# A decoder of attentions and routed experts: the combine stages are folded into the attentions that follow

## The chip, the cores and the metric

The kernel runs on one core of a Trainium2 chip as one launch. The metric is the device time of that launch in microseconds (us), the median of several executions. Engines are named as the profile does: PE is TensorE, PEld its weight load, DVE is VectorE, ACT is ScalarE, POOL is GpSimd, and SP is the queue that issues most DMAs. "L712" is line 712 of the kernel before.

## What is computed

`x` is 16 batches of 112 tokens with 256 channels, and `ctx` has 375 context tokens for each batch. Eight blocks follow each other, each added to `x`:

```
x = x + attention_L0(layernorm(x), ctx)   # 16 heads of 16, biases, a mask of keys for each query
x = x + experts_L0(layernorm(x))          # 2 of 8 experts per token, relu
x = x + attention_L1(layernorm(x), ctx)   # one head of 256, relu in place of softmax
x = x + block_L1(layernorm(x))            # y = layernorm(x) + causal self attention with rotary
                                          # angles; y + 2 of 8 experts, capacity 448, gelu
x = x + attention_L2(layernorm(x), ctx)   # 16 heads of 64, no biases
x = x + experts_L2(layernorm(x))          # 1 of 8 experts per token, relu
x = x + attention_L3(layernorm(x), ctx)   # 16 heads of 64, biases, output bias of 256
x = x + experts_L3(layernorm(x))          # all 16 experts and a shared one, weighted
```

An expert layer's output for a token is the sum of its chosen experts' rows, each times the token's gate.

## The kernel before

`x` stays in SBUF as 112 partitions by 16 batches by 256. Each stage is an `nc.Block()`: every engine runs its own list of instructions for the stage, ordered against the others by counting semaphores alone, and no engine goes into the next block before all have left this one.

The stages of an expert layer of L0, L1 and L2 are three. `route` normalises, scores and picks experts, computes for each token its place in a table of slots (`core.slot_out`) and its gate (`core.gate`), and POOL scatters the normalised rows to `slots_in` in DRAM. `expert_tiles` runs the experts over tiles of slots and stores the results to `slots_out`. `combine` gathers them back: for each of 16 batches POOL issues one indirect DMA (L1548) per chosen expert into one of 8 `got` buffers, and DVE multiplies by the gate and adds to `x` (L1559). Ahead of L2 and L3, SP also loads the next attention's four weights of 1 MB in `combine` (L1539), into buffers that live for `combine` and the attention only.

`cross_attention` serves L0 (narrow: heads of 16) and L2 and L3 (wide: heads of 64). Its unit is a step of one batch, in 16 sub-steps of one head. In the step of batch b, PE computes the scores of each head, transposes the probabilities of three heads back ("turn", L508), multiplies them with the values (L523), and puts a piece of other work in between, from a table written out by hand (`order`): keys K0 to K7, values V0 to V5 and queries of batch b+1, and the output projection Y0 and Y1 of batch b-1 (L459). With an output bias, PE adds it as one more matmul of a row of ones with the bias row (L462). DVE takes each head's maximum (L826), ACT the exponent (L676), POOL the reciprocal of the sum and the product (L710, L712). At sub-step 0 DVE runs `normalise_start` of batch b+1 (L741 to L745), and then the lower halves of K0 and K1 (L770), for which PE's K2 waits in sub-step 1; POOL raises the variance to -1/2 (L704, L732), and `normalise_end` is in sub-step 2. Ahead of the first step of a wide attention DVE splits the weights (L918, L920) and two contexts (L808, L810) into high and low halves.

`relu_attention` has shorter steps: DVE normalises batch b+1 (L978 to L982, POOL L1801, DVE L1931) at the step's start, while PE computes scores of b and keys of b+1 (L1815); then PE transposes the normalised tokens (L1823).

In `self_attention`'s step DVE does, in this order: `divide(b-1)`, `group_max(b, 2)`, `spread_keys(b+1)` (L2320), `norm_3(b+2)` (L2285), `group_max(b, 3)` (L2328), and the rest. `norm_3` writes the normalised tokens that PE transposes at L2068; ACT's exponents (L2233) of group 3 wait for the last maximum.

Most batches of these three functions run in hardware loops of two batches a turn (`Fori`); the first and the last ones are written out.

Of the kernel before, what the change touches and what calls it, by code (L numbers as in the profile page):

```python
# [123 lines left out]
def cross_attention(nc, core, name, ctx_in, w, dh, mask=None):  # L124
# [39 lines left out]
    with ctx:  # L164
# [82 lines left out]
        nweights = 4 + (4 if biased else 0) + (3 if mask else 0)  # L247
# [63 lines left out]
        def run(heads, first, last, tail, engine):  # L311
# [11 lines left out]
        with nc.Block() as block:  # L323

            @block.sync
            def _(sp):
# [3 lines left out]
                if biased:  # L330
                    for dst, src in ((bq, w["bq"]), (bk, w["bk"]), (bv, w["bv"]), (bo, w["bo"])):
                        sp.dma_start(dst[:, :], src).then_inc(weights.sem, 16)
# [9 lines left out]
                if wide:  # L342
# [10 lines left out]
                    with sp.Fori(0, (B - 2) // 2) as i:  # L353
                        next_ctx(Batch(i, 2))
                        next_ctx(Batch(i, 3))
# [31 lines left out]
                with sp.Fori(0, (B - 2) // 2) as i:  # L387
                    spread(Batch(i, 0))
                    next_load(Batch(i, 2))
                    spread(Batch(i, 1))  # L390
                    next_load(Batch(i, 3))
                spread(Batch(0, B - 2))
                spread(Batch(0, B - 1))
# [4 lines left out]
            def _(pe):  # L398
                def piece(p, b, slot):
# [53 lines left out]
                    else:  # L453
# [4 lines left out]
                        for c in range(EC):  # L458
                            ins = pe.matmul(bank[0:T, 0:YW], oT[:, c, :], wo[:, c, m * YW:(m + 1) * YW],  # L459
                                            start=(c == 0), stop=(c == EC - 1 and not biased))  # L460
# [141 lines left out]
                pe.wait_ge(weights.sem, weights.at(16 * nweights))  # L602
# [9 lines left out]
            def _(act):  # L612
                act.preload_act_table(ACT.Exp)

                act.wait_ge(weights.sem, weights.at(16 * nweights))
# [84 lines left out]
            def _(pool):  # L700
# [5 lines left out]

                def weigh(b, h):
# [21 lines left out]
                with pool.Fori(0, B - 1) as i:  # L729

# [1866 lines left out]
```

## Time and profile before

| | us |
|---|---|
| median of 3 runs | 3820.91 (3817.61 to 3829.95) |
| the profiled execution's own time | 3808.83 |
| its span, first to last instruction | 3807.0 |
| PE busy | 3181.0 (84%) |
| DVE busy | 1563.8 (41%) |
| ACT busy | 1538.9 (40%) |
| POOL busy | 1223.3 (32%) |

The profile is of one execution. The busy share of an engine is a mean over stages with different limits, so stages are read one by one. In the rows below, times are from the span's start; what stands in brackets at a row's end is the idle time of the engine before it, and what ended that time.

### The profile page before, as it was taken

How to read it: one execution, taken by the hardware profiler on the slowest of the kernel's cores; microseconds unless marked ns; L12 is line 12 of the kernel's file. 1: busy time of each engine (PE TensorE's matmuls, PEld its weight loads, DVE VectorE, ACT ScalarE, POOL GpSimd, SP SyncE). 2: the span in 40 equal slices, each digit the busy share in tenths (PEclk: the TensorE clock that was granted, in tenths of full speed). 3: DMA queues.
4: the chain of work that ended last, by engine and by line, in shares of the span. 5: the costliest groups of instructions: out<-in, count | busy, mean ns of one | idle time of the engine just before them, and what ended most of it. 6: DMA issues, size and time to landing. Idle time of an engine off the chain costs nothing. (4 is left out here: it accounts for less than half of the span.)

```text
span 3807.0 us, 67515 instructions
## 1 busy us (share of the span) xinstructions
PE 3181.0 (84%) x22302; PEld 2618.4 (69%) x22302; DVE 1563.8 (41%) x3515; ACT 1538.9 (40%) x4385; POOL 1223.3 (32%) x1334
## 2 busy tenths in 40 slices
PE   2899927993978837948999999759599999996998
PEld 2777727883856625636888888648478888885998
DVE  2777730002456530024444444310244444444776
ACT  1555513441345522214555555324255555552222
POOL 0000030003000030034676676510166666664121
PEclk8999958997989958978999999779799999996999
DMA  6555418982100014330000000058400000000001
GB/s 181 129 130 138 104 37 291 321 307 73 44 13 0 0 35 144 115 93 17 9 12 8 8 8 5 3 204 311 132 10 8 8 8 12 8 1 14 26 26 33
DMA packets 155225, 287.93 MB, mean 76 GB/s; under 512 B 53214, under 2 KB 126876, under 8 KB 137244
## 3 DMA queue, kind: packets, MB, share of 16 engines
q1 hardware_dynamic: 147420, 267.93, 23.1%
q0 software_dynamic: 7680, 18.36, 1.8%
q8 instruction: 75, 1.23, 0.1%
q14 instruction: 50, 0.41, 0.0%
HBM read 240.88 MB, written 45.35 MB: 75 GB/s over the span
## 5 line engine op out<-in xcount | busy, mean ns | idle before, releaser
L712 POOL TENSOR_SCALAR L_probs<-L_probs,L_inverse 112x375 f32<-112x375 f32 x512 | 645.7, 1261 | 87.1 <-issue 87.1
L826 DVE TENSOR_REDUCE L_negmax<-bank 112x1 f32<-112x375 f32 x768 | 394.7, 542 | 427.2 <-PE bank L481 361.4
L676 ACT ACTIVATE L_probs<-bank,L_negmax 112x375 f32<-112x375 f32 x768 | 434.5, 571 | 204.9 <-DVE L_negmax L826 199.7
L508 PE MATMUL bank<-ident,L_probs 112*125 112x112 f32 x2304 | 400.6, 283 | 17.6 <-POOL L_probs L712 11.3
L508 PEld LDWEIGHTS bank<-ident,L_probs 112*125 112x125 f32 x2304 | 336.3, 188 | 93.0 <-issue 62.0
L710 POOL TENSOR_TENSOR L_inverse<-L_sums,neg_one 112x1 f32<-112x1 f32 x512 | 308.1, 602 | 256.4 <-ACT L_probs L676 256.4
L656 ACT ACTIVATE L_probsT<-bank 125x336 f32<-125x336 f32 x512 | 231.6, 452 | 263.0 <-PE bank L508 263.0
L638 ACT ACTIVATE v<-bank 125x512 f32<-125x512 f32 x192 | 114.7, 598 | 266.1 <-PE bank L431 266.1
L523 PE MATMUL bank<-L_probsT,v 125*64 125x112 f32 x3072 | 206.1, 270 | 1.1 <-ACT L_probsT L656 1.1
L523 PEld LDWEIGHTS bank<-L_probsT,v 125*64 125x64 f32 x3072 | 150.8, 137 | 30.7 <-DVE L_oT L842 2.0
L1484 ACT ACTIVATE L0t_hidden<-bank,L0t_b 128x128 f32<-128x128 f32 x280 | 102.8, 367 | 165.3 <-PE bank L1444 146.1
L1444 PE MATMUL bank<-L0t_xT,L0t_w 128*128 128x128 f32 x1120 | 134.2, 279 | 22.9 <-DMA L0t_b<-in_F_b 22.5
L676 ACT ACTIVATION_READ_ACCUMULATOR L_probs<-bank,L_negmax 112x1 f32 x768 | 152.7, 199 | 0.0
L1444 PEld LDWEIGHTS bank<-L0t_xT,L0t_w 128*128 128x128 f32 x1120 | 130.3, 194 | 31.7 <-issue 31.0
L424 PE MATMUL bank<-L_ctx_hi,L_wk_hi 128*128 128x376 f32 x512 | 146.9, 368 | 3.3 <-DVE L_keys_lo L770 3.0
L1505 DVE TENSOR_TENSOR L0t_ys<-bank,L0t_b 128x256 f32<-128x256 f32 x35 | 14.8, 424 | 314.3 <-PE bank L1456 314.3
L431 PE MATMUL bank<-L_wv_hi,L_ctx_hi 128*125 128x512 f32 x384 | 137.9, 440 | 0.0
L770 DVE SCALAR_TENSOR_TENSOR L_keys_lo<-bank,L_bk,L_keys_hi 128x376 fp32r<-128x376 f32 x128 | 76.6, 608 | 141.1 <-ACT L_keys_hi L628 141.0
L732 POOL TENSOR_TENSOR L_stats<-L_stats,neg_half 112x1 f32<-112x1 f32 x15 | 8.1, 542 | 381.5 <-DVE L_stats L745 381.5
L459 PE MATMUL bank<-wo,L_oT 128*112 128x128 f32 x1024 | 128.7, 281 | 1.6 <-DVE L_oT L842 0.8
L424 PE MATMUL bank<-L_ctx_hi,L_wk_lo 128*128 128x376 f32 x512 | 129.8, 334 | 0.0
L416 PE MATMUL bank<-L_hT,wq 128*128 128x112 f32 x1024 | 128.4, 280 | 1.0 <-ACT L_hT L626 1.0
(291 smaller groups left out, 6995.8 us busy)
## 6 DMA issues: line engine op xcount, KB each, us to landing
L0t_w<-in_F_w SPq DMA_DIRECT2D x70, 1024.0 KB, 5.3
L2t_w<-in_F_w SPq DMA_DIRECT2D x42, 1024.0 KB, 5.2
L_keys<-spread_k SPq DMA_DIRECT2D x64, 376.0 KB, 6.4
L_ctxT<-in_ctxT SPq DMA_DIRECT2D x48, 375.0 KB, 3.3
L1t_w<-in_F_w SPq DMA_DIRECT2D x16, 1024.0 KB, 6.1
slots_in<-zeros SPq DMA_DIRECT2D x4, 1792.0 KB, 16.5
L_q<-spread_q SPq DMA_DIRECT2D x128, 56.0 KB, 2.2
spread_k<-L_k_hi SPq DMA_DIRECT2D x16, 376.0 KB, 2.5
```

What stands on the lines that cost most here:

```text
L416: ins = pe.matmul(bank[:, (c - 4 * m) * T:(c - 4 * m + 1) * T], wq[:, k, c * P:(c + 1) * P], hT[:, k, :], start=(k == 0), stop=(k == DC - 1))
L424: ins = pe.matmul(bank[:, 0:SP], wt[:, k, m * P:(m + 1) * P], c[b.par][:, k, :], start=(n + k == 0), stop=(n + k == DC + 1))
L431: ins = pe.matmul(bank[0:SJ, 0:VW], c[b.par][:, k, j * SJ:(j + 1) * SJ], wt[:, k, vn * VW:(vn + 1) * VW], start=(n + k == 0), stop=(n + k ...
L459: ins = pe.matmul(bank[0:T, 0:YW], oT[:, c, :], wo[:, c, m * YW:(m + 1) * YW], start=(c == 0), stop=(c == EC - 1 and not biased))
L508: ins = pe.transpose(psT[h % len(psT)][0:SJ, j * T:(j + 1) * T], probs[h % NB][:, j * SJ:(j + 1) * SJ], core.ident[0:T, 0:T])
L523: ins = pe.matmul(bank[i * dh:(i + 1) * dh, at:at + T], v[b.par][0:SJ, j, (h + i) * dh:(h + i + 1) * dh], probsT[(h + i) % NT][:, j, :], s ...
L656: act.activation(probsT[h % NT][:, :, :], psT[h % len(psT)][0:SJ, 0:J * T].rearrange("p (j t) -> p j t", t=T), ACT.Copy)\
L676: act.activation(probs[e % NB][:, :], psS[e % 2][0:T, 0:S], ACT.Exp, bias=negmax[b.par][:, e:e + 1], accum_out=sums[b.par][:, e:e + 1]).th ...
L710: pool.tensor_tensor(inverse[b.par][:, h:h + 1], sums[b.par][:, h:h + 1], core.neg_one[0:T, :], ALU.pow)
L712: pool.tensor_scalar(probs[h % NB][:, :], probs[h % NB][:, :], inverse[b.par][:, h:h + 1], None, ALU.mult)\
L826: dve.tensor_reduce(negmax[b.par][:, h:h + 1], psS[h % 2][0:T, 0:S], AX, ALU.max, negate=True).then_inc(maxed.sem, 1)
L1444: ins = pe.matmul(psH[f % 4][:, 0:tile], w1[t.par][:, k, f * P:(f + 1) * P], xT[:, k, :], start=(k == 0), stop=(k == DC - 1))
```

## The change

- `combine` is gone, three stages in all. `relu_attention` and the wide `cross_attention` gather and add themselves: four `got` buffers, the gathers of four batches at the start of the stage, then the gathers of batch b+4 in step b (in `relu_attention` behind the power of b, in a wide attention ahead of head 8). DVE's `add_experts` adds a batch's rows directly ahead of that batch's `normalise_start`. An attention L2 step so has two more indirect DMAs on POOL and two more DVE operations, an L3 step one of each.
- The 4 MB of weights of the next wide attention are loaded in `route` of the expert layer before, behind its own loads, into buffers held from there on, with a counter of their own.
- The output bias of L0 and L3 is broadcast to 112 partitions when it is loaded, and POOL adds it to `x` (`bias_x`), once a batch: in L3 ahead of head 5 and in L0 behind the next batch's power. The matmuls L462 go; DVE's addition of Y waits for `x_biased`. POOL waits for the stage's weights first where there are biases.
- In `self_attention`, `norm_3(b+2)` stands directly behind `divide(b-1)`.
- The loops of `cross_attention`, `relu_attention` and `self_attention` are written out for all 16 batches (not POOL's loop in `self_attention`).

```diff
@@ cross_attention
-            bo = sb("bo", [1, D])
+            bo = sb("bo", [T, D])
+            x_biased = core.counter("x_biased")
+        if wide:
+            wide_weights = core.counter("wide_weights")
+            got = [sb(f"got{r}", [T, topk, D]) for r in range(4)]
...
-            with engine.Fori(0, (B - 4) // 2) as i:
-                heads(Batch(i, 1), False, False)
-                heads(Batch(i, 2), False, False)
-            heads(Batch(0, B - 3), False, False)
+            for n in range(1, B - 2):
+                heads(Batch(0, n), False, False)
...
-                        if biased:
-                            ins = pe.matmul(bank[0:T, 0:YW], core.ones[0:1, 0:T], bo[0:1, m * YW:(m + 1) * YW],
-                                            start=False, stop=True)
...
+                def bias_x(b):
+                    pool.wait_ge(normed_ready.sem, normed_ready.at(b.n + 1))
+                    xb = core.x[:, b.n, :]
+                    pool.tensor_tensor(xb, xb, bo[:, :], ALU.add).then_inc(x_biased.sem, 1)
...
+                        if h == 5 and biased:
+                            bias_x(b)
+                        if h == 8 and b.n + 4 < B:
+                            gather(b.n + 4)
                         weigh(b, h)
+                def gather(n):
+                    if n >= 4:
+                        pool.wait_ge(added.sem, added.at(n - 3))
+                    for k in range(topk):
+                        pool.indirect_dma_start(
+                            out=got[n % 4][:, k, :], out_offset=None, in_=core.slots_out[:, :],
+                            in_offset=bass.IndirectOffsetOnAxis(ap=core.slot_out[:, k, n:n + 1], axis=0))\
+                            .then_inc(gathered[n % 4].sem, 16)
+                if biased:
+                    pool.wait_ge(weights.sem, weights.at(16 * nweights))
                 if wide:
+                    for n in range(4):
+                        gather(n)
                     run(heads, rstd, None, lambda b: None, pool)
...
+                def add_experts(n):
+                    dve.wait_ge(gathered[n % 4].sem, gathered[n % 4].at(16 * topk * (n // 4 + 1)))
+                    for k in range(topk):
+                        ins = dve.scalar_tensor_tensor(out=core.x[:, n, :], in0=got[n % 4][:, k, :],
+                                                       scalar=core.gate[:, k, n:n + 1], in1=core.x[:, n, :],
+                                                       op0=ALU.mult, op1=ALU.add)
+                        if k == topk - 1:
+                            ins.then_inc(added.sem, 1)
+                        dve.drain()
                 def normalise_start(b):
+                    if wide:
+                        add_experts(b.n)
                     dve.bn_stats(stats[:, 0:6], x_of(b))
...
@@ route, sync
+                for dst, s in next_loads:
+                    sp.dma_start(dst, s).then_inc(core.counter("wide_weights").sem, 16)
@@ combine
-def combine(nc, core, name, topk, next_loads=()):
...
@@ self_attention, vector
                     if prior:
                         divide(b + -1)
+                    if after2:
+                        norm_3(b + 2)
                     group_max(b, 2)
                     if after:
                         spread_keys(b + 1)
-                    if after2:
-                        norm_3(b + 2)
                     group_max(b, 3)
```

`relu_attention` gets the same `gather` and `add_experts`, and calls `add_experts(b.n + 1)` ahead of `normalise_start`.

## Rows read from the trace of the kernel before

**Rows 1.** A stretch of time by engine: busy (instructions), TensorE clock, DMA share, GB/s.

```profile
200.00:460.00 260.00, 237.50 (x2228) 193.84 (x2227) 197.00 (x467) 140.33 (x430) 5.41 (x10) 1.00 0.55 130
1120.00:1320.00 200.00, 176.04 (x983) 121.47 (x981) 120.66 (x266) 114.33 (x502) 12.44 (x23) 0.93 0.00 0
1800.00:2100.00 300.00, 300.00 (x2359) 245.82 (x2358) 136.69 (x275) 159.30 (x441) 207.79 (x227) 1.00 0.03 9
```

**Rows 2.** Order of time, border from the first combine to relu attention: start, length.

```profile
867.32 0.96 POOL L1548 DMA_INDIRECT L0c_got<-slots_out,slot_out  x1 [293.93 <-PEq L1534]
...
910.03 0.35 SPq L1781 DMA_DIRECT2D L1x_wq<-in_X_wq  x1
...
920.76 1.59 PE L1815 MATMUL bank<-L1x_ctxT,L1x_wk 128*128 128x375 f32 x2 [56.91 <-DMA L1x_ctxT<-in_ctxT]
```

**Rows 3.** Order of time, border from the second combine to attention L2.

```profile
1667.30 0.37 SPq L1539 DMA_DIRECT2D v<-in_L_wk  x1
...
1712.13 14.73 SPq L344 DMA_DIRECT2D L_ctxT<-in_ctxT  x3
...
1726.02 0.42 DVE L741 BATCH_NORM_STATS2 L_stats<-x 112x6 f32<-112x256 f32 x1
```

**Rows 4.** Order of time, border from the third combine to attention L3.

```profile
2692.11 0.35 SPq L1539 DMA_DIRECT2D v<-in_L_wk  x1
...
2714.94 0.33 SPq L332 DMA_DIRECT2D L_bq<-in_L_bq  x1
```

**Rows 5.** Instructions on the second combine's tile: ns min/median/max, first and last start.

```profile
L1548 POOL DMA_INDIRECT L1c_got<-slots_out,slot_out x32: 929/934/1136, 1668.0 to 1707.0; - x32
L1559 DVE SCALAR_TENSOR_TENSOR x<-L1c_got,gate,x x32: 475/484/542, 1676.7 to 1711.1; 112x256 f32<-112x256 f32 x32
```

**Rows 6.** One line's instructions, attention L2, the batches inside the loop.

```profile
L741 DVE BATCH_NORM_STATS2 L_stats<-x x11: 415/417/419, 1838.9 to 2274.2; 112x6 f32 x11
```

**Rows 7.** The same line, attention L3, the batches inside the loop.

```profile
L741 DVE BATCH_NORM_STATS2 L_stats<-x x11: 415/416/418, 2847.0 to 3294.0; 112x6 f32 x11
```

**Rows 8.** Order of time, VectorE, a batch of attention L2 outside the loop.

```profile
2361.22 0.41 DVE L741 BATCH_NORM_STATS2 L_stats<-x 112x6 f32<-112x256 f32 x1
```

**Rows 9.** Order of time, TensorE, output projection in attention L3.

```profile
3002.35 1.26 PE L459 MATMUL bank<-wo,L_oT 128*112 128x128 f32 x10
...
3003.94 0.58 PE L508 MATMUL bank<-ident,L_probs 112*125 112x112 f32 x3
```

**Rows 10.** Order of time, TensorE, output projection in attention L0.

```profile
295.95 1.03 PE L459 MATMUL bank<-L_wo,L_oT 128*112 128x256 f32 x4
...
297.52 0.37 PE L494 MATMUL bank<-L_barred,ident_b 112*112 112x376 bf16 x1
```

**Rows 11.** Order of time, VectorE, start of a batch's step in attention L2.

```profile
2013.78 0.15 DVE L745 TENSOR_SCALAR L_stats<-L_stats 112x1 f32<-112x1 f32 x1
2014.31 1.18 DVE L770 SCALAR_TENSOR_TENSOR L_keys_lo<-bank,L_keys_hi 128x376 fp32r<-128x376 f32 x2 [0.38 <-ACT L_keys_hi L628]
```

**Rows 12.** The same moment on TensorE.

```profile
2015.36 0.61 PE L424 MATMUL bank<-L_ctx_hi,L_wk_hi 128*128 128x376 f32 x2
```

**Rows 13.** Order of time, one step of relu attention.

```profile
958.40 0.41 DVE L1931 TENSOR_SCALAR L1x_normed<-x,L1x_stats 112x256 f32 x1 [0.65 <-POOL L1x_stats L1801]
...
960.03 0.36 PE L1823 MATMUL bank<-ident,L1x_normed 112*128 112x112 f32 x2
```

**Rows 14.** Order of time, one step of self attention at full clock.

```profile
1246.78 0.41 DVE L2285 TENSOR_SCALAR L1s_normed<-y,L1s_stats 112x256 f32 x1
...
1247.42 0.38 PE L2068 MATMUL bank<-ident,L1s_normed 112*128 112x112 f32 x2 [1.62 <-DVE L1s_normed L2285]
...
1247.75 0.35 ACT L2233 ACTIVATE L1s_probs<-bank,L1s_negmax 112x112 f32<-112x112 f32 x1 [1.12 <-DVE L1s_negmax L2328]
```

**Rows 15.** GpSimd's line in attention L2's last batch.

```profile
L710 POOL TENSOR_TENSOR L_inverse<-L_sums,neg_one x16: 567/568/572, 2405.2 to 2434.4; 112x1 f32<-112x1 f32 x16
```

**Rows 16.** GpSimd's groups: busy us, mean ns; idle before.

```profile
L1621 POOL TENSOR_TENSOR L3d_w_lo<-L3d_raw,L3d_w_hi 128x768 fp32r<-128x768 f32 x18 | 33.6, 1869 | 2.6
```

More of the change, by code:

```diff
@@ L246, in cross_attention @@
         taken = {c: core.counter(f"taken_{c}") for c in "LQKVOY"}
-        nweights = 4 + (4 if biased else 0) + (3 if mask else 0)
+        nweights = (0 if wide else 4) + (4 if biased else 0) + (3 if mask else 0)
+        if wide:
+            wide_weights = core.counter("wide_weights")
+            got = [sb(f"got{r}", [T, topk, D]) for r in range(4)]
+            gathered = [core.counter(f"gathered{r}") for r in range(4)]
+            added = core.counter("added")
         if wide:
@@ L352, in _ @@
                     next_ctx(Batch(0, 1))
-                    with sp.Fori(0, (B - 2) // 2) as i:
-                        next_ctx(Batch(i, 2))
-                        next_ctx(Batch(i, 3))
+                    for n in range(2, B):
+                        next_ctx(Batch(0, n))
                     return
@@ L386, in _ @@
                 load(Batch(0, 1))
[L387 to L393, printed above, removed]
+                for n in range(B):
+                    spread(Batch(0, n))
+                    if n + 2 < B:
+                        next_load(Batch(0, n + 2))
                 sp.wait_ge(core.zeroed_sem, 16 * (core.slots_in.shape[0] // (B * T)))
@@ L728, in _ @@
                 rstd(Batch(0, 0))
-                with pool.Fori(0, B - 1) as i:
-                    pool.wait_ge(var_ready.sem, var_ready.at(i + 2))
-                    pool.tensor_tensor(stats[:, 9:10], stats[:, 8:9], core.neg_half[0:T, :], ALU.pow)\
-                        .then_inc(rstd_ready.sem, 1)
+                for n in range(B):
+                    if n + 1 < B:
+                        rstd(Batch(0, n + 1))
+                    bias_x(Batch(0, n))
             @block.vector
@@ L776, in take @@
                     dve.wait_ge(made[p[0]].sem, made[p[0]].at(count(p, b)))
+                    if p[0] == "Y" and biased:
+                        dve.wait_ge(x_biased.sem, x_biased.at(b.n + 1))
                     if p[0] == "Y":
@@ L943, in cross_attention @@
             w_split.stage_over(2)
+            wide_weights.stage_over(64)
+            added.stage_over(B)
+            for r in range(4):
+                gathered[r].stage_over(16 * topk * (B // 4))
             ctx_split.stage_over(B)
@@ L1750, in relu_attention @@
         weightsT = sb("weightsT", [SJ, J, T])
+        got = [sb(f"got{r}", [T, topk, D]) for r in range(4)]
+        gathered = [core.counter(f"gathered{r}") for r in range(4)]
+        added = core.counter("added")
         weights = core.counter("weights")
@@ L1768, in run @@
             heads(Batch(0, 0), False)
-            with engine.Fori(0, (B - 2) // 2) as i:
-                heads(Batch(i, 1), False)
-                heads(Batch(i, 2), False)
+            for n in range(1, B - 1):
+                heads(Batch(0, n), False)
             heads(Batch(0, B - 1), True)
@@ L1926, in _, with add_experts @@
                 dve.wait_ge(weights.sem, weights.at(16 * len(loads)))
+                def add_experts(n):
+                    dve.wait_ge(gathered[n % 4].sem, gathered[n % 4].at(16 * topk * (n // 4 + 1)))
+                    for k in range(topk):
+                        ins = dve.scalar_tensor_tensor(out=core.x[:, n, :], in0=got[n % 4][:, k, :],
+                                                       scalar=core.gate[:, k, n:n + 1], in1=core.x[:, n, :],
+                                                       op0=ALU.mult, op1=ALU.add)
+                        if k == topk - 1:
+                            ins.then_inc(added.sem, 1)
+                        dve.drain()
                 def normalise_end(b):
@@ L1973, in relu_attention @@
             s.stage_over(16 * B // 2)
+        added.stage_over(B)
+        for s in gathered:
+            s.stage_over(16 * topk * (B // 4))
         for s in (var_ready, rstd_ready, normed_ready, scored, mixed, made["L"], taken["L"], made["Q"], taken["Q"],
@@ L2034, in run @@
             heads(Batch(0, 0), False, True, True, True)
-            with engine.Fori(0, (B - 4) // 2) as i:
-                heads(Batch(i, 1), True, True, True, True)
-                heads(Batch(i, 2), True, True, True, True)
-            for n in range(B - 3, B):
+            for n in range(1, B):
                 heads(Batch(0, n), True, n + 1 < B, n + 2 < B, n + 3 < B)
```

124 lines of the change are left out of this document (55 added, 69 removed).

## The prediction

> **What bounds the kernel now.** I read the kernel by stages, first by stretches of time. In the steady part of the wide attentions PE is busy all the time at the full clock, 300 us of 300 [rows 1]; in attention L0 it is busy 237.5 of 260 us, and in self attention 176 of 200 with a granted clock of 0.93 [rows 1]. So work taken from PE counts there, and work given to DVE or POOL costs only what makes PE wait. Then I read the borders in order of time. A combine stage leaves PE idle: it had waited 56.9 us when relu attention's first matmul started [rows 2]. The reader should see that no other work lies beside a combine, so its whole length, border included, is on the path.
>
> **What is removed.** From the first gather of the first combine (867.32) to relu attention's first load (910.03) is 42.7 us [rows 2]; from SP's first weight load (1667.30) to L2's first context load (1712.13), 44.8 [rows 3]; for the third, 22.8 [rows 4]. Together -110.3. The 4 MB of weights move to `route`, behind its own loads on SP's queue, and are needed over 200 us later; I cost them at nothing. Their cover is `route`, where PE and DVE work on data in SBUF; without it they would cost what their bytes take.
>
> The bias matmuls L462. In L3 the last of ten projection matmuls ends at 3003.61, and the next work starts at 3003.94 [rows 9]; matmuls in a row start before the one ahead ends, so at least 0.33 us per piece goes. From the other side, an L3 batch takes (3294.0 - 2847.0) / 10 = 44.70 us and an L2 batch (2274.2 - 1838.9) / 10 = 43.53 [rows 6, 7]: 1.17 for two pieces, but L3's other biases are in it. I take the middle, 0.46: 32 pieces, -14.7 (bounds -10.6 and -18.7). In L0 the gap behind four matmuls is 297.52 - 296.98 = 0.54 [rows 10], up to 0.80 with one matmul's share of the 1.03; at 0.6 it is -9.6 for 16 batches. Bounds are 0, if the queries' way through DRAM and not PE sets L0's step, and -12.8.
>
> **What is added at the starts.** A gather takes POOL (1707.0 - 1668.0) / 31 = 1.26 us and a DVE addition 0.48, two with what lies between them about 1.1 [rows 5]. Eight gathers are 10.1 us of POOL. In relu attention PE started 10.7 us after the stage [rows 2], so the first power, behind them in POOL's queue, is about in time, and the addition lies under the first keys. The gathers' 0.9 MB share the DMA engines with some 1.8 MB of loads: 0 to +5.4 (10.7 x 0.9 / 1.8); I take +1.5, since a queue of many small loads rarely fills them. In L2 and L3 the normalisation starts 13.9 us after the stage (1726.02 - 1712.13) [rows 3], and the gathers are over by then; the additions stand on the path: +1.1 in L2, +0.6 in L3, and +0.3 for the wider bias load. Sum +3.5.
>
> **What is added to the steps.** Wide attention: DVE's additions stand ahead of `normalise_start`, and behind that stands the lower half of K0, for which PE's K2 waits. L745 ends at 2013.93; the two L770 start at 2014.31, so the first ends near 2014.90, and K2 starts at 2015.36 [rows 11, 12]. Shifted by 1.12, DVE is free at 2015.05 and K0 done at 2015.64; with the 0.23 us that PE starts after DVE's end where it does wait (1247.19 to 1247.42 [rows 14]), or a third of that where only its queue waits, K2 starts at 2015.7 to 2015.9. I take +0.35 for 14 batches, +4.9; L3, with one addition, +0.1, +1.4 (bounds 0, and the whole 1.12 and 0.56: +23.5). What is late next is all behind K2, since PE has no idle time to give back.
>
> POOL in a wide step needs (2434.4 - 2405.2) / 15 = 1.95 us a head [rows 15], 31.1 a batch; with the power of the variance (0.57, as L710) and two gathers (2.5) 34.2 of 43.5. A product is needed three heads, some 8 us, later; behind the gathers wait heads 8 and 9, 2.5 us late. Hidden. Only in the last batch, where PE has no pieces left, POOL runs without a pause and sets the pace [rows 15]; L3's `bias_x` stands there. No row shows an addition of 112x256 on POOL: bounds are 0.57 (112x1, L710) and 1.87 (128x768, L1621 [rows 16]); in proportion 1.0. So +1.0.
>
> Relu attention: the normalised tokens are ready at 958.81, PE takes them at 960.03 [rows 13]; less 0.23, the slack is 0.99 against the addition's 1.12: +0.13, +2 for 15 batches (bounds 0, +16.8).
>
> Self attention: PE waits 1.62 us for `norm_3` [rows 14]. But ahead of the second maximum it delays that maximum, the exponents, the queries and `spread_keys` by about 0.35 (its start to the next operation's), and the last maximum gets the same 0.35 back; ACT's exponents, which wait for that maximum [rows 14], start when they did. ACT then runs through to the tokens that PE's next projection needs, so PE's wait moves instead of going. What may go is the low clock: 0.93 over 200 us means 28 us at 1.2 GHz [rows 1], at most 14 us lost over the stretch and 16 over the stage. I take -3 (bounds +5, -16).
>
> Loops: a batch outside the loop starts (2361.22 - 2274.2) / 2 = 43.5 after the one before, like inside [rows 6, 8]. Cost 0. The Trainium skill, in Runtime: NRT & Kernel Launch, "Instruction fetch mechanics", says that a taken branch can force a fetch before execution goes on, and that kernels prefer unrolling. By it the loops' edges would hold something to win; the rows show none, so the sum stays.
>
> **The sum.** -110.3 - 14.7 - 9.6 + 3.5 + 4.9 + 1.4 + 1.0 + 2 - 3 = -124.8, from the profiled execution's own 3808.8 to 3684. The median of the runs lies 12.1 above that execution; taken from it, the forecast is 3696 us.
>
> **Rivals.**
> (a) The additions stand on the path in full, since DVE's order, not the slack, decides: relu 16.8 and wide 23.5 instead of 8.3, +32: 3728. For it: DVE's operations wait for PE and ACT at many places of a step. Against: PE's full use is at the matmuls' own pace, and DVE is busy 137 of 300 us [rows 1]. 0.12.
> (b) POOL becomes the wait in the wide steps. It decides from 8 us of delay, that is if a pair of gathers cost 8 instead of 2.5; then heads 8 and 9 hold up PE. At 10 us, in L3 with `bias_x` in it, 2 us for 12 batches and two stages: +48, 3744. Against: 0.93 us each, with DVE at work beside them, and at most 1.14 [rows 5]. 0.04.
> (c) DVE locks POOL out at the start of a wide stage. DVE splits weights and contexts there; if each gather waits for what DVE runs, POOL's queue grows from 10.1 by DVE's some 11 us of work to 21, and the first power comes 5 us late in L2 and 2 in L3: 3703. The Trainium skill, SBUF — State Buffer, "Who interferes with whom", says that a DVE copy or cast in two-port mode keeps GpSimd from writing descriptors; by its example of 3.1 us instead of 0.62, eight gathers would take 25 us, an estimate, and L2 start 9 us late. No row here shows gathers beside casts. 0.06.
> (d) The clock in self attention comes back in full, since PE's longest wait in the step goes: -13 more: 3683. 0.13.
> (e) The bias matmuls' time isn't won, since POOL's `x_biased` or L0's other chain takes their place: +24: 3720. 0.07.
> (f) Slower than before: written-out code is fetched too late. 62 batches leave their loops (12 in four stages, 14 in relu attention), so it decides from 125 / 62 = 2.0 us per batch more; at 3 us it is +186: 3882. Against it the batches outside the loop [rows 8]. 0.02.
> The forecast has 0.56.
>
> **How the numbers follow.** Its own range is 3680 to 3712: L0's and L3's bounds down, half of the steps' upper bounds up. With (a), (d), (e) and (c) inside, 3674 to 3730 leaves out about 2 in 10, with the spread of the runs. Under 0.3% (11 us), about what a measurement of this kernel can tell from no change, only (f) comes near: faster 0.97, same 0.01, slower 0.02.
>
> **What would show it.** PE's gap at the three borders: about 15, 22 and 22 us. L741's spacing: about 43.9 in L2 and 43.9 in L3, so nearly alike; above 44.5 in L2 speaks for (a). L0's steps 0.6 shorter. POOL's gathers near 0.93 in the first 15 us of L2; over 2 for (c). Self attention's clock over 0.93 for (d), and the wait at L2068 gone while one at L2077 comes. Wrong would be made the forecast by a new wait of over 1 us in each wide step, since there are 30.

## The result and the profile after

The changed kernel takes 3703.0 us (median of 4 runs, 3701.7 to 3705.0), beside 3819.3 for the kernel before on the same chip: a ratio of 0.970, 95% interval 0.968 to 0.972. The prediction was 3696 (3674 to 3730), faster with 0.97. The profiled execution has a span of 3703.1 us, 103.9 less than before.

I cut both traces at TensorE's first and last matmul of each stage (in attention L0 at the first batch's first scores matmul). The two columns are single executions.

| part | before | after | change | predicted |
|---|---|---|---|---|
| attention L0 | 413.5 | 410.8 | -2.7 | -9.6 |
| routing's last matmul to the end of L0's expert tiles | 338.8 | 352.5 | +13.7 | 0 |
| border to relu attention | 56.9 | 15.0 | -41.9 | -41.2 |
| relu attention | 146.8 | 147.9 | +1.1 | +2 |
| self attention | 268.4 | 254.8 | -13.6 | -3 |
| border to L2 | 65.0 | 21.9 | -43.1 | -43.7 |
| attention L2 | 718.7 | 727.5 | +8.8 | +4.9 |
| routing's last matmul to the end of L2's tiles | 207.6 | 214.5 | +6.9 | 0 |
| border to L3 | 44.6 | 24.8 | -19.8 | -21.9 |
| attention L3 | 738.9 | 721.7 | -17.2 | -12.3 |
| all others | | | +3.9 | 0 |

The borders came as forecast: "about 15, 22, 22" were 15.0, 21.9 and 24.8. Three lines were not: L0 gained little, self attention much, and the expert tiles, in which nothing was changed, took 20.6 us more.

Stretches of time of the changed kernel, the counterparts of [rows 1] (us busy, instructions; then the clock, the DMA engines' share and GB/s):

```profile
200.00:460.00 260.00, 231.89 (x2215) 191.98 (x2214) 197.35 (x470) 140.32 (x430) 13.18 (x21) 1.00 0.56 132
1090.00:1290.00 200.00, 177.01 (x1071) 124.86 (x1070) 126.73 (x282) 122.75 (x550) 12.96 (x24) 1.00 0.00 1
1750.00:2050.00 300.00, 298.87 (x2342) 244.81 (x2342) 137.47 (x287) 158.87 (x441) 217.41 (x240) 1.00 0.06 16
```

In self attention the granted clock is now 1.00, where it was 0.93: that is 2.4 GHz all the time. In L2 PE is idle 1.1 of 300 us, where it had not been idle at all.

The start of a batch's normalisation on VectorE in steady L2 and L3 (ns min/median/max, first and last start), the counterparts of [rows 6, 7]:

```profile
L779 DVE BATCH_NORM_STATS2 L_stats<-x x14: 427/428/429, 1716.4 to 2285.5; 112x6 f32<-112x256 f32 x14
```

```profile
L779 DVE BATCH_NORM_STATS2 L_stats<-x x13: 427/428/429, 2760.5 to 3282.9; 112x6 f32<-112x256 f32 x13
```

L2's step is (2285.5 - 1716.4) / 13 = 43.78 us, +0.25 against 43.53. L3's is (3282.9 - 2760.5) / 12 = 43.53, -1.17 against 44.70.

The border to relu attention in order of time, beside [rows 2]:

```profile
878.49 0.96 POOL L1806 DMA_INDIRECT L1x_got<-slots_out,slot_out  x1 [307.32 <-POOLq L1414]
...
888.21 1.05 DVE L1949 SCALAR_TENSOR_TENSOR x<-L1x_got,gate,x 112x256 f32<-112x256 f32 x2 [12.61 <-DMA L1x_maskT<-in_X_maskT]
...
890.09 2.21 PE L1832 MATMUL bank<-L1x_ctxT,L1x_wk 128*128 128x375 f32 x3 [15.05 <-DMA L1x_ctxT<-in_ctxT]
```

Eight gathers take 9.7 us (878.49 to 888.13), each 0.93 to 0.96, and VectorE's additions end at 889.26, before the first keys' matmuls, which wait for the context's load: the addition is under cover, as the prediction had it.

The border to L2, beside [rows 3]. This is where rival (c) is to be looked for:

```profile
1625.30 1.23 DVE L960 CAST L_wk_hi<-v 128x2048 fp32r<-128x2048 f32 x1 [3.77 <-PEq L1414]
1625.98 1.38 POOL L738 DMA_INDIRECT L_got<-slots_out,slot_out  x1 [236.30 <-POOLq L1414]
1626.61 2.29 DVE L962 TENSOR_TENSOR L_wk_lo<-v,L_wk_hi 128x2048 fp32r<-128x2048 f32 x1
...
1630.46 2.77 POOL L738 DMA_INDIRECT L_got<-slots_out,slot_out  x1 [0.30 <-issue]
...
1635.24 0.93 POOL L738 DMA_INDIRECT L_got<-slots_out,slot_out  x1 [0.31 <-issue]
...
1638.14 0.55 DVE L848 CAST L_ctx_hi<-L_ctxT 128x752 fp32r<-128x752 f32 x1 [4.02 <-DMA L_ctxT<-in_ctxT]
...
1639.63 1.05 DVE L769 SCALAR_TENSOR_TENSOR x<-L_got,gate,x 112x256 f32<-112x256 f32 x2
...
1642.93 0.60 PE L410 MATMUL bank<-ident,L_normed 112*128 112x112 f32 x2 [21.87 <-DVE L_normed L788]
```

A gather's issue takes 1.38 us, 2.49 and 2.77 while VectorE splits weights, and 0.93 when VectorE waits (1635.24). So the mechanism of (c) is there: "over 2 for (c)" came true. Its price did not: TensorE starts 21.9 us after the tiles, as forecast without it. The power on GpSimd comes at 1641.77, right behind VectorE's statistics; what is late is VectorE, which waits 4.02 us for the second context, ahead of the first batch's addition. The Trainium skill, SBUF — State Buffer, "Who interferes with whom", says that VectorE and GpSimd share a port pair under an exclusive lock. That gathers get longer beside VectorE's work agrees with it (2.77 beside 0.93); the lock itself no trace here shows.

The border to L3, beside [rows 4]:

```profile
2624.20 0.35 SPq L337 DMA_DIRECT2D L_bq<-in_L_bq  x1
...
2625.54 0.43 SPq L337 DMA_DIRECT2D L_bo<-in_L_bo  x1
2626.02 18.19 SPq L349 DMA_DIRECT2D L_ctxT<-in_ctxT  x3
2629.16 1.23 DVE L960 CAST L_wk_hi<-v 128x2048 fp32r<-128x2048 f32 x1 [7.11 <-DMA L_bo<-in_L_bo]
...
2642.07 0.55 DVE L848 CAST L_ctx_hi<-L_ctxT 128x752 fp32r<-128x752 f32 x1 [3.90 <-DMA L_ctxT<-in_ctxT]
...
2643.56 0.48 DVE L769 SCALAR_TENSOR_TENSOR x<-L_got,gate,x 112x256 f32<-112x256 f32 x1
...
2646.30 0.60 PE L410 MATMUL bank<-ident,L_normed 112*128 112x112 f32 x2 [24.82 <-DVE L_normed L788]
```

VectorE's first split waits for L_bo, the bias row broadcast to 112 partitions: it starts 3.1 us after the issue of the context's load (2626.02), where the kernel before had it 0.9 after (2716.63 and 2717.52 in its trace). That is 2.2 us for which I had 0.3.

### The profile page after: what moved, and what is told of

The parts are those of the page before. It is cut to its first block and busy times, and to the rows that moved or that the text cites. A ratio compares the mean times of both kernels' runs of the same rounds, so it can differ in the third digit from the quotient of the medians.

```text
span 3703.1 us, 62003 instructions
## 1 busy us (share of the span) xinstructions
PE 3152.0 (85%) x22206; PEld 2606.9 (70%) x22206; DVE 1554.8 (42%) x3515; ACT 1537.1 (42%) x4385; POOL 1248.5 (34%) x1366
## 5 line engine op out<-in xcount | busy, mean ns | idle before, releaser
L718 POOL TENSOR_TENSOR L_inverse<-L_sums,neg_one 112x1 f32<-112x1 f32 x512 | 297.0, 580 | 147.2 <-ACT L_probs L678 146.7
L706 POOL TENSOR_TENSOR L_stats<-L_stats,neg_half 112x1 f32<-112x1 f32 x48 | 26.9, 561 | 538.8 <-DVE L_stats L783 538.8
L738 POOL DMA_INDIRECT L_got<-slots_out,slot_out x48 | 57.4, 1196 | 442.5 <-POOLq L1414 236.3
L521 PEld LDWEIGHTS bank<-L_probsT,v 125*64 125x64 f32 x3072 | 152.4, 138 | 30.4 <-ACT L_probsT L658 1.6
L1806 POOL DMA_INDIRECT L1x_got<-slots_out,slot_out x32 | 30.5, 953 | 315.3 <-POOLq L1414 307.3
## 6 DMA issues: line engine op xcount, KB each, us to landing
slots_in<-zeros SPq DMA_DIRECT2D x4, 1792.0 KB, 16.3
```

The source lines that it names most:

```text
L521: ins = pe.matmul(bank[i * dh:(i + 1) * dh, at:at + T], v[b.par][0:SJ, j, (h + i) * dh:(h + i + 1) * dh], probsT[(h + i) % NT][:, j, :], s ...
L718: pool.tensor_tensor(inverse[b.par][:, h:h + 1], sums[b.par][:, h:h + 1], core.neg_one[0:T, :], ALU.pow)
```

## The experiments

Twelve runs, one of them (e5) of the changed kernel again. "Ratio" is to the kernel before on the same chip, with its 95% interval; the changed kernel's own is 0.9697 (0.9678 to 0.9716). Since the runs used several chips, differences between kernels are taken from the ratios, times 3819 us. The stages are cut as in the table.

**e1, norm_3 back.** The last edit of the diff undone:

```
+                    group_max(b, 2)
+                    if after:
+                        spread_keys(b + 1)
                     if after2:
                         norm_3(b + 2)
-                    group_max(b, 2)
-                    if after:
-                        spread_keys(b + 1)
```

> The changed kernel with one edit undone: in self attention's step norm_3 stands behind spread_keys again. In the traces the self attention stage took 268.4 us from its first to its last matmul before the change and 254.8 after it, 13.6 less, and the granted clock had no dip in it afterwards. Theory (the move gives the clock back): the stage goes back to about 268, dips of the clock return, and the time is about 13 us above the changed kernel's 3703, so 3716. Rival (the dips of the kernel before were chance, or came from what ran ahead of the stage, so the move gives only what I forecast for it, 3 us): the stage takes about 258 and the time is 3706.

3711.2 us, ratio 0.9730 (0.9714 to 0.9747), so 12.6 us slower than the change, though the two intervals still touch; the stage takes 265.3. A stretch of its self attention:

```profile
1100.00:1300.00 200.00, 175.23 (x1011) 122.56 (x1010) 120.84 (x263) 117.05 (x521) 11.89 (x22) 0.95 0.00 1
```

0.95 where the change has 1.00. In the clock's record of this kernel eight dips of 3.4 us to half speed lie inside the stage, and seven with two of 6.8 in the kernel before; the changed kernel has none after the first 30 us. The theory holds, rival (d) of the prediction. What a dip costs is read from the steps of one batch. Two steps of this kernel without a dip:

```profile
1250.67 0.41 PE L2098 MATMUL bank<-ident,L1s_normed 112*128 112x112 f32 x2 [1.58 <-DVE L1s_normed L2315]
...
1266.00 0.41 PE L2098 MATMUL bank<-ident,L1s_normed 112*128 112x112 f32 x2 [1.57 <-DVE L1s_normed L2315]
```

Such a step takes 15.33 us, and one with a dip in it some 16.55, so eight dips are about 10 us. The stage is 10.5 longer than the change's; its steps without a dip are longer too (e12), and against that its clock was low for a shorter time near the start.

**e12, the same edit alone on the kernel before.**

> The kernel before with one part of the change alone: norm_3 first in self attention's step. Undone in the changed kernel, it cost 10.5 us of that stage (254.8 to 265.3), with the granted clock down from 0.98 to 0.94. Theory: self attention goes from 268.4 to about 256 us, the clock in its steady part from 0.93 to 0.98, and the time from 3819 to 3807. Rival (the clock's gain needed something else of the change, as what runs ahead of the stage): 265 us, 3816.

3811.6 us, ratio 0.9968 (0.9944 to 0.9992): 12 us faster, with an interval of 3 to 21 that holds both the theory's 12 and the rival's 4. Its stage took 264.7 in the profile, which is the rival's number, but not for the rival's reason:

```profile
1145.00:1345.00 200.00, 173.35 (x1054) 122.36 (x1053) 123.52 (x267) 122.81 (x546) 11.89 (x22) 1.00 0.00 0
```

The steady part is at 1.00, without a dip. A part of what it lost lies at the stage's ends, 17.1 us of 1.2 GHz near the start and 9.1 at the end. Another part lies in the steps. The weight loads of the two transposes of each step, in e12 and in the change (ns min/median/max, first and last start):

```profile
L2068 PEld LDWEIGHTS bank<-ident,L1s_normed x24: 138/143/146, 1147.7 to 1315.4; 112*128 112x128 f32 x24
```

```profile
L2098 PEld LDWEIGHTS bank<-ident,L1s_normed x22: 139/140/141, 1104.8 to 1254.9; 112*128 112x128 f32 x22
```

That is (1315.4 - 1147.7) / 11 = 15.25 us a step in e12, which keeps the loops, and (1254.9 - 1104.8) / 10 = 15.01 in the change, where they are written out; with the old order a step without a dip is 15.33 written out (e1, e3) and 15.26 to 15.35 in loops (the kernel before). In the eleven executions with the new order the stage took 254.2 to 264.7 us, in the three with the old one 264.5 to 268.4. So the move takes away the dips in the middle, some 10 us, and together with the written-out loops 0.3 us of each step; the ends vary.

**e3, the kernel before, written out.** Every loop as in this pattern, nothing else:

```
-            with engine.Fori(0, (B - 4) // 2) as i:
-                heads(Batch(i, 1), False, False)
-                heads(Batch(i, 2), False, False)
-            heads(Batch(0, B - 3), False, False)
+            for n in range(1, B - 2):
+                heads(Batch(0, n), False, False)
```

> The kernel before with one part of the change alone: all loops of the three cross attentions, relu attention and self attention written out. Theory as in my prediction: a loop's edge costs nothing, so the wide attentions' steps stay at 43.5 and 44.7 us. What the traces of the change suggest besides: the code's transfers disturb L0, whose step becomes uneven (24.7 to 26.3 in place of 25.4), so the time is 0 to 8 us above the 3819 of the kernel before. Open is the stage of L0's expert tiles, 274.4 us before and 287.7 after the change, though nothing in it was changed: if the length of the program is the cause it shows here too (+13, and +7 in L2's tiles), about 3840; if it is where the combine's removal left the stage, or chance of a run, it does not.

3829.6 us, ratio 1.0037 (1.0024 to 1.0051): +14. The wide steps stay at 43.5 and 44.7, relu attention at 147.3 (146.8). L0 goes from 413.5 to 419.8, with steps of 25.4 to 26.8 where each had been 25.4. The tiles took 348.1 and 212.3 in the profile, 9 and 5 more; e5 below says what to make of that.

**e2, e9, e10, attention L0 in loops again:** all of it (e2), SyncE's part alone (e9), the four computing engines' alone (e10). The edit is the one above, backwards, only where the attention isn't a wide one.

> The changed kernel with attention L0 alone in loops again (all its engines and the DMA queue's part); everything else as changed. In the traces a step of L0 takes 25.4 us before, always; after the change between 24.7 and 26.3, mean 25.3, and TensorE waits for the queries' transfer in some steps. Theory (the code fetched from DRAM shares the DMA engines with the queries' and keys' way through DRAM, and eats what the bias matmuls gave back): with the loops back every step takes about 24.8, the stage gets some 7 us shorter, and the time is about 3696. Rival (the queries' way through DRAM sets the step whatever the loops do, the lower bound that I had kept for this term): steps stay near 25.3 and the time stays at 3703.

> The changed kernel with only the DMA queue's part (SyncE) of attention L0 in a loop again; TensorE, VectorE, ScalarE and GpSimd stay written out. So far the kernels with L0 wholly written out took 347 to 354 us (eight of them) from the routing's last matmul to the end of L0's expert tiles, those with loops 339 and 343. Theory (the engines' code, 23 fetches of 16 KB in 320 us against 5, makes L0's steps uneven): L0 stays uneven with 24.7 to 26.5 us a step and the stage at 411 to 415 us; SyncE's own code is a small part. The tiles' 9 us go with whatever SyncE left in its instruction buffer: 343 here, and the time is about 3694. Rival (they go with the engines' code): 351, 3703.

> The changed kernel with the four computing engines' part of attention L0 in loops again, and SyncE's written out: the other half of the run with only SyncE's loop. Theory: L0's steps are even, 24.9, and the stage takes 408; the tiles take 351 (if their 9 us go with SyncE's code), so 3700. Rival (both go with the engines' code): 408 and 343, 3688, like the kernel with all of L0 in loops. If neither half brings the tiles back to 343, chance made the difference.

| | time | ratio | L0 | L0's tiles |
|---|---|---|---|---|
| the change | 3703.0 | 0.9697 | 410.8 | 352.5 |
| e2, all | 3686.2 | 0.9662 (0.9646 to 0.9678) | 408.2 | 342.6 |
| e9, SyncE | 3702.2 | 0.9694 (0.9673 to 0.9716) | 412.5 | 350.9 |
| e10, engines | 3692.6 | 0.9673 (0.9653 to 0.9692) | 404.7 | 351.5 |

e2 gained 13 us where the theory had 7, and only 2.6 of them lie in L0 in its profile; e9 came out as its rival said, and e10 between its theory and its rival, with neither half bringing the tiles back to 343.

The queue with instructions between 110 and 430 us (packets, MB, share of the 16 DMA engines), of the change and of e10:

```profile
q8 instruction: 23, 0.38, 0.5%
```

```profile
q8 instruction: 5, 0.08, 0.1%
```

23 transfers of 16 KB against 5, the number of the kernel before. And what TensorE waits for in L0, in the change (us in all, times, longest):

```profile
PE bank L410 <- DVE L_normed L788: 7.0, 9, 0.8
...
PE bank L492 <- DMA L_q<-spread_q: 3.4, 4, 1.4
```

The second row is new: four times the queries are not back from DRAM, by up to 1.4 us. In e10 the same wait is 0.5 us, once. The steps of e10, by VectorE's first operation of each:

```profile
L788 DVE BATCH_NORM_STATS2 L_stats<-x x11: 415/418/419, 179.9 to 429.3; 112x6 f32 x9, 112x6 f32<-112x256 f32 x2
```

(429.3 - 179.9) / 10 = 24.94, against (433.7 - 181.1) / 10 = 25.26 in the change. So L0's part goes with the computing engines' loops: with the bias on GpSimd, the seven executions with these engines written out took 410.8 to 415.1 (mean 412.4), the three with them in loops 404.7 to 408.2 (mean 406.1), 6 us less. That it is the code's transfers that delay the queries fits the waits and is not shown; they take 0.5% of the DMA engines' time. SyncE's loop alone does nothing to L0, nor to the tiles.

**e5, the change once more.**

> The changed kernel, nothing altered, to see what repeats. From the end of the routing's matmuls to the end of L0's expert tiles it took 352 us here against 339 before the change; two more kernels with attention L0 written out took 352 and 353, one 348, and one with its loops 343. Theory (the expert tiles' transfers keep no fixed pace, and chance makes most of the 13 us): this execution gives another value, anywhere from 340 to 355. Rival (the value belongs to the program): 352 again, within 1. In both the time is 3703, and self attention takes 255 with a clock of 0.98 in its steady part.

3699.7 us, ratio 0.9697 (0.9675 to 0.9720); L0's tiles 347.2, L2's 210.7. The rival is out: the same program gave 352.5 and 347.2. e12 says it more clearly. Up to the tiles it has the same code as the kernel before, whose 338.8 I had compared everything with, and took 347.1. So up to 8 of the 13.7 us are the chance of one execution. The rest leans towards the loops: the four executions with all of L0 in loops gave 338.8, 342.6, 347.1 and 346.9 (mean 343.9), the ten others 347.2 to 354.0 (mean 351.1), and these 7 us are about what e2's 13 and e3's 14 leave beside L0's 6. But neither half of the loops brings them back (e9, e10), and what would need both stays open. L2's tiles took 206.9 to 218.2, in no order.

**e4, the bias matmuls back,** in L0 and L3, and GpSimd's addition gone:

```
-                                            start=(c == 0), stop=(c == EC - 1))
+                                            start=(c == 0), stop=(c == EC - 1 and not biased))
+                        if biased:
+                            ins = pe.matmul(bank[0:T, 0:YW], core.ones[0:1, 0:T], bo[0:1, m * YW:(m + 1) * YW],
+                                            start=False, stop=True)
...
-                        if h == 5 and biased:
-                            bias_x(b)
```

> The changed kernel with the output bias added on TensorE again (one short matmul per piece) and no addition on GpSimd. Theory by the traces: L3's step goes from 43.5 back to 44.7 us (16 of them: +18), L0's from 25.3 to 25.4 or a little more (+2): about 3723. Rival (my sum: 0.46 us a piece in L3 and 0.3 in L0): +24, with L0's steps 0.6 longer: 3727. Second rival (the wait moves to GpSimd's addition and nothing is won by the edit): 3703.

3723.1 us, ratio 0.9750 (0.9734 to 0.9767): 20 us slower. L3's steps in it:

```profile
L769 DVE BATCH_NORM_STATS2 L_stats<-x x13: 427/428/429, 2769.9 to 3306.5; 112x6 f32<-112x256 f32 x13
```

(3306.5 - 2769.9) / 12 = 44.72, 1.19 above the change, so the 1.17 us a step are all the matmuls' (some 0.59 for each piece). The whole stage is 737.2, 15.5 more, since the steps at its ends don't lengthen. L0's stage is 417.6, 6.8 more. L3's border is 22.2 here, since the small bias load is back.

**e8, the combines back.** The three stages as before, no gathers or additions in the attentions; the wide weights stay in the routing.

> The changed kernel with the three combine stages back and no gathers or additions in the attentions; the wide weights are still loaded in the routing stages. Theory (the borders in the traces: 56.9 against 15.0, 65.0 against 21.9 and 44.6 against 24.8 us, less what the additions cost inside the attentions, 9 in L2, 2 in L3, 1 in relu attention): +105 - 12 = +93, so 3796. Rival (the weights' loads were what lengthened the second and third combine, so that with them out of the way the combines are shorter): the second costs 32 gathers at 1.26 us all the same, 40, the third only 16 at 1.0, so some 5 less: 3791.

3797.9 us, ratio 0.9951 (0.9934 to 0.9968), 97 us slower than the change. The borders are 57.3, 65.1 and 46.6, where the kernel before, with the weights' 4 MB beside the second and third, has 56.9, 65.0 and 44.6. So the weights cost a combine nothing; the third's 2.0 us more fit the wider bias row, which this kernel keeps. Nor do they cost the routing stages more than 1.8 us where they are now, borders included. L2's tiles, which follow, spread too widely (206.9 to 218.2, against 207.6 to 212.3 with the weights in the combine) to exclude 2 us there. L2's steps without the additions:

```profile
L770 DVE BATCH_NORM_STATS2 L_stats<-x x13: 415/415/419, 1847.5 to 2369.9; 112x6 f32<-112x256 f32 x13
```

(2369.9 - 1847.5) / 12 = 43.53: the +0.25 of L2's step belongs to what moved into it.

**e6, the additions elsewhere in the step,** where VectorE is idle for 3.4 us:

```
-                    if wide:
-                        add_experts(b.n)
...
                         if h == (4 if wide else 6) and not b_first:
                             divide(b + -1, NG - 1)
+                        if wide and h == 4 and b.n + 2 < B:
+                            add_experts(b.n + 2)
```

> The changed kernel with the experts' additions of the wide attentions moved within the step: VectorE adds the rows of batch b + 2 at head 4 of step b, where it is idle for 3.4 us, and no longer those of batch b + 1 ahead of the normalisation at head 0. Theory (the additions are 0.27 us a step late in L2 and 0.1 in L3, as the steps of 43.8 against 43.5 us say): L2's steps go back to 43.5, L3's to 43.4, the time to about 3698. Rival (what lengthens L2's step is GpSimd, which comes back to its heads 5 to 6 us late after the gathers at head 8, since its drain waits for them): the steps stay at 43.8, 3703.

```profile
L777 DVE BATCH_NORM_STATS2 L_stats<-x x14: 415/416/419, 1718.7 to 2284.8; 112x6 f32<-112x256 f32 x14
```

(2284.8 - 1718.7) / 13 = 43.55, and L2's stage 721.6 (727.5 and 725.0 in the two executions of the change). The gathers are where they were, so the rival, GpSimd, is out for the step. L3 stays at 43.5: its one addition had cost nothing. The time doesn't show it: 3701.9, ratio 0.9692 (0.9674 to 0.9710), L2's tiles having taken 218.2 in the profile.

**e7, another order at the start of L2 and L3:**

```
                         split_ctx(b)
-                        split_ctx(b + 1)
                     normalise_start(b)
                     normalise_end(b)
+                    if wide:
+                        split_ctx(b + 1)
...
-                    for n in range(4):
-                        gather(n)
+                    gather(0)
+                    gather(1)
+                    def first(b):
+                        rstd(b)
+                        gather(2)
+                        gather(3)
```

> The changed kernel with another order at the start of L2 and L3: VectorE adds and normalises batch 0 before it splits the context of batch 1, for which it waited 3.9 us, and GpSimd gathers for batches 0 and 1, makes the power for batch 0, and gathers for 2 and 3 only then. In the trace of the change the gathers beside VectorE's splitting of weights take up to 2.8 us in place of 0.93, the addition starts at 1639.6 and the first matmul at 1642.9. Theory (VectorE's order is what sets the start): the first matmul comes about 4 to 5 us earlier in each of L2 and L3, and if the second context is not late for it the time is 3694. Rival (the keys of batch 0 or the second context set the start): TensorE starts earlier and waits later by as much, 3703.

The start of L2 in it:

```profile
1641.59 1.05 DVE L774 SCALAR_TENSOR_TENSOR x<-L_got,gate,x 112x256 f32<-112x256 f32 x2
...
1642.74 0.43 DVE L784 BATCH_NORM_STATS2 L_stats<-x 112x6 f32<-112x256 f32 x1
...
1644.90 0.61 PE L410 MATMUL bank<-ident,L_normed 112*128 112x112 f32 x2 [16.30 <-DVE L_normed L793]
```

The addition follows the first context's split; TensorE's gap at the border is 16.3 us instead of 21.9, and 19.5 instead of 24.8 in L3. The stages themselves get no longer (724.4 and 720.7). 3686.8 us, ratio 0.9657 (0.9636 to 0.9677): 15 us by the ratios, 11 of them from the borders and the rest within the spread. The edit moves VectorE's order and GpSimd's together, so it doesn't say what each is worth.

**e11, the four together:** L0 in loops, e6, e7, and the broadcast bias behind the first context on a counter of its own.

```
+                def load_bo():
+                    if biased:
+                        sp.dma_start(bo[:, :], w["bo"].rearrange("a d -> (a d)").partition_broadcast(T))\
+                            .then_inc(bo_here.sem, 16)
...
                     pool.wait_ge(normed_ready.sem, normed_ready.at(b.n + 1))
+                    pool.wait_ge(bo_here.sem, bo_here.at(16))
```

> The changed kernel with four edits: attention L0 in loops, the wide attentions' additions at head 4 for batch b + 2, the reordered start of L2 and L3, and the broadcast load of the output bias behind the first context on a counter of its own, for which only GpSimd's bias addition waits (in L3 VectorE's first operation came 3.1 us after the first context load's issue, in the kernel before 0.9). Theory: each keeps its gain, -13 for the loops, -4 for the additions, -11 for the starts, -2 for the bias load, from 3703: 3673, with L3's border at about 17 us. Rival (the gains are in part chance of the expert tiles, which take 347 to 354 and 209 to 218 us whatever is done): 3683.

3672.2 us (3667.0 to 3679.5), ratio 0.9616 (0.9600 to 0.9632): 31 us below the change, as expected. VectorE at the border to L3 in it, beside the one above:

```profile
2596.72 0.42 DVE L1583 TENSOR_TENSOR L2t_ys<-bank,L2t_b 128x256 f32<-128x256 f32 x1 [7.27 <-PE bank L1534]
2601.92 1.36 DVE L987 CAST L_wk_hi<-v 128x2048 fp32r<-128x2048 f32 x1 [4.77 <-DMA L_bv<-in_L_bv]
...
2610.99 0.48 DVE L792 SCALAR_TENSOR_TENSOR x<-L_got,gate,x 112x256 f32<-112x256 f32 x1
...
...
2614.49 0.55 DVE L869 CAST L_ctx_hi<-L_ctxT 128x752 fp32r<-128x752 f32 x1 [0.90 <-DMA L_ctxT<-in_ctxT]
```

The first split comes 5.2 us after the tiles' last operation and waits for the small bias; it was 7.5. The border is 17.2 us.

## Why the prediction was right, and where not

The combines, -110.3 + 3.5 for the starts: right. The three borders gave -104.8, e8 puts the whole at 97 net of what the attentions then carry. The weights cost the routing nothing that the runs can tell. Two terms of the starts were mis-sized: the wider bias load, +2.2 for +0.3, and L2's first two steps, which I had not counted: they took 30.6 and 45.0 us against 28.5 and 40.8 (30.4 and 43.6 in e5). One piece of it is a wait for GpSimd:

```profile
1697.29 0.92 PE L506 MATMUL bank<-ident,L_probs 112*125 112x112 f32 x3 [1.90 <-POOL L_probs L720]
```

The bias matmuls, -14.7 in L3: in a steady step the upper bound was the true one, 1.17, since the other biases in L3's step cost nothing, but 16 of them overstate the stage, which e4 puts at 15.5. In L0, -9.6: with even steps it is (25.4 - 24.94) x 16 = 7.4; the stages in loops say 7.0 (413.5 and 412.7 with the matmuls, 404.7, 405.3 and 408.2 without). The change itself got -2.7, for the reason below. Rival (e) is out by e4. GpSimd's addition of 112x256, sized 1.0 us between 0.57 and 1.87, takes 0.738 (a line's group: busy us, mean ns):

```profile
L713 POOL TENSOR_TENSOR x<-x,L_bo 112x256 f32<-112x256 f32 x16 | 11.8, 738 | 0.0
```

The steps, +0.35 in L2 and +0.1 in L3: the mechanism held, at 0.25 and 0. VectorE in a step of L2, and TensorE at that moment, beside [rows 11, 12]:

```profile
1978.02 1.04 DVE L769 SCALAR_TENSOR_TENSOR x<-L_got,gate,x 112x256 f32<-112x256 f32 x2
...
1979.92 0.15 DVE L783 TENSOR_SCALAR L_stats<-L_stats 112x1 f32<-112x1 f32 x1
1979.99 0.99 DVE L808 SCALAR_TENSOR_TENSOR L_keys_lo<-bank,L_keys_hi 128x376 fp32r<-128x376 f32 x2
```

```profile
1980.58 0.62 PE L425 MATMUL bank<-L_ctx_hi,L_wk_hi 128*128 128x376 f32 x2 [0.16 <-DVE L_keys_lo L808]
```

The two additions push the statistics back, the keys' lower halves start right behind them, and K2 waits 0.16 us for these. e6 shows the cause. Rival (a), the whole 1.12 us a step, is out, and so is (b): GpSimd did come back late, and it was hidden in all steps but the first.

Self attention, -3: the size was wrong by 10 us, and rival (d) right. The prediction's waits are there, beside [rows 14]:

```profile
1239.89 0.38 PE L2098 MATMUL bank<-ident,L1s_normed 112*128 112x112 f32 x2 [0.93 <-issue]
...
1242.90 1.97 PE L2107 MATMUL bank<-L1s_wqkv,L1s_hT 128*112 128x512 f32 x4 [0.56 <-ACT L1s_hT L2239]
```

The 1.62 us of L2068 became 0.93 (L2098) and 0.56 at the projection (L2107): "the wait moves instead of going". But with the wait in one piece the granted clock dipped in most steps, and with it divided in none of the steady part; I had given that no more than 0.13. That the division is what does it is my reading of these runs, which changed the order and nothing else. The 0.3 us that a step without a dip also lost (15.33 to 15.01, in written-out code alone) was in no term.

The loops, 0: this is the step that failed. "A batch outside the loop starts 43.5 after the one before" was read in L2, where the DMA engines are at 0.03 of their time, and carried to L0, where they are at 0.55 [rows 1]. e3 charges the writing out 14 us; 6 of them are L0's, and 7 more may be L0's tiles (e5). What tells L0 from L2 is not shown: their DMA load differs, and so does much else. In self attention, with the new order, written-out steps are 0.24 us shorter (e12). The sentence of the Trainium skill that I weighed (Runtime: NRT & Kernel Launch, "Instruction fetch mechanics": kernels prefer unrolling) points the other way than e3's 1.0037 for the whole kernel; its section's 16 KiB blocks agree with the 23 packets and 0.38 MB. Rival (f), 2 us for each batch, is out.

That the forecast came within 7 us of the median has luck in it. 10.6 us too little for self attention and 4.9 in L3 (2 of these because that execution of the kernel before had 738.9 in L3 where e3 and e12 have 736.9 and 736.3) stand against 6.9 in L0, 3.9 in L2 and 2.1 at L3's border. The tiles' 20.6 us are in no term; but the 12.1 us that I added because the profiled execution lay below its median cover more than half of them, since its short tiles were a part of why it lay there.

## What to carry to other kernels

A stage that only gathers and adds is worth its whole length when the next stage has room; but order the consumer's first batch so that its engine doesn't wait for the second batch's load ahead of it. Price written-out code in the stage that gets it and not in another one: here it cost 6 us in L0, whose data go through DRAM, and nothing in L2 and L3. A step's bias matmul is best priced by the whole stage, ends included. And before a difference in an untouched stage is explained, look at several executions of the same code: here one had been 8 us below another.

## What the runs showed of the hardware

A drain on GpSimd behind a gather seems to wait until the gather has landed. GpSimd at head 8 of a step in L2, and the gathers' times to landing there (us min/median/max):

```profile
1998.24 1.02 POOL L738 DMA_INDIRECT L_got<-slots_out,slot_out  x1 [0.16 <-issue]
1999.57 0.94 POOL L738 DMA_INDIRECT L_got<-slots_out,slot_out  x1 [0.31 <-issue]
2000.53 1.03 POOL L718 TENSOR_TENSOR L_inverse<-L_sums,neg_one 112x1 f32<-112x1 f32 x1
2003.27 1.24 POOL L720 TENSOR_SCALAR L_probs<-L_probs,L_inverse 112x375 f32<-112x375 f32 x1 [1.71 <-issue]
```

```profile
L738 POOL DMA_INDIRECT L_got<-slots_out,slot_out x2: 938/978/1017, 1998.2 to 1999.6; - x2
...
DMA to landing us min/median/max: 3.4/3.4/3.5
```

The second gather is issued at 1999.57 and lands 3.46 later, at 2003.03; the product of the probabilities, which stands behind a drain, starts at 2003.27. It starts 0.24 us after the last landing in all 12 such steps of L2 and 0.20 after it in all 12 of L3. The two gathers thus hold GpSimd's heads up by some 4.3 us, where I had counted 2.5. I had not foreseen it; TensorE waited 1.9 us for it in this execution, once. A kernel without the drain was not run, so the cause rests on these 24 landings.

Beside VectorE's splits of 128x2048 a gather's issue takes up to 2.96 us in place of 0.93. Low clock in the steady part of self attention came as dips of mostly 3.4 us, at most one in a step, with TensorE's wait of 1.6 us in one piece, and not with 0.93 and 0.56; a dip of 3.4 us cost its step 1.2 us (e1).
